# A decoder layer: self-attention's probabilities divided on Vector ahead of their transposes, and the reciprocals of cross-attention moved ahead of two maxima

## What is computed

```python
q = _apply_rope((x @ Wq.T) ...); k = _apply_rope((x @ Wk.T) ...); v = (x @ Wv.T) ...
scores = jnp.einsum('bhqd,bhkd->bhqk', q, k) / np.sqrt(HEAD_DIM)
scores = jnp.where(causal, scores, -jnp.inf)
attn = jax.nn.softmax(scores, axis=-1)
out = jnp.einsum('bhqk,bhkd->bhqd', attn, v)
return out ... @ Wo.T          # then x1 = layernorm(x + this)
```

## Time and profile before

| | |
|---|---|
| median of 3 runs | 1928.02 us (1926.51 to 1933.37) |
| the profiled execution | 1933.5 us, span 1931.7 us |
| busy share of the span | PE 85%, DVE 74%, ACT 73%, POOL 44% |
| self-attention | from 0 to about 638 us |
| cross-attention | to about 1385 us |
| feed-forward | to the end |

### The profile page before, as it was taken

How to read it: one execution, slowest core, us unless ns; L and a number is a source line. 1 busy time by engine, 2 the same in 40 slices (tenths; PEclk the granted TensorE clock), 3 DMA queues, 4 the chain that set the end, 5 groups by cost and what they waited for, 6 DMA issues and landing times. The chain is left out here.

```text
span 1931.7 us, 43922 instructions
## 1 busy us (share of the span) xinstructions
PE 1649.0 (85%) x12964; PEld 904.5 (47%) x13028; DVE 1433.1 (74%) x1915; ACT 1405.0 (73%) x2861; POOL 852.0 (44%) x1378
## 2 busy tenths in 40 slices
PE   5999999999996499999999999998247777777776
PEld 4777777777775133333333333333013333333332
DVE  3555555555554588999999999997558999999986
ACT  4555555555553187888888888887539999999996
POOL 3466565665663322323222323232464554555442
PEclk8999999999998598999999999998668888888887
DMA  3334334334333563444444444444332333333321
GB/s 114 101 97 124 113 110 125 108 111 129 103 114 112 102 188 102 117 109 125 108 110 118 117 116 108 120 109 149 100 96 88 99 109 101 102 110 98 98 66 44
DMA packets 118566, 211.02 MB, mean 109 GB/s; under 512 B 32097, under 2 KB 34689, under 8 KB 116737
## 3 DMA queue, kind: packets, MB, share of 16 engines
q1 hardware_dynamic: 110338, 209.51, 38.4%
q0 software_dynamic: 8192, 1.07, 0.3%
HBM read 133.41 MB, written 76.02 MB: 108 GB/s over the span
## 5 line engine op out<-in xcount | busy, mean ns | idle before, releaser
L926 DVE TENSOR_REDUCE b_smax<-b_m 128x2 f32<-128x1024 f32 x512 | 612.3, 1223 | 75.8 <-PE b_m L981 71.3
L901 ACT ACTIVATE b_prob<-b_e 128x512 f32<-128x512 f32 x1024 | 556.4, 599 | 104.1 <-PE b_e L1028 88.2
L1028 PE MATMUL b_e<-b_xs,b_cs 50*128 50x512 f32 x1024 | 331.0, 479 | 19.5 <-ACT b_prob L901 11.6
L1011 PE MATMUL b_av<-b_prob,b_vT 128*32 128x256 f32 (+1 forms) x3584 | 318.9, 428 | 3.3 <-ACT b_prob L901 0.5
L981 PE MATMUL b_m<-b_cs,b_xs 48*128 48x512 f32 x1024 | 286.5, 445 | 35.9 <-DMA b_gamma<-in_gamma 29.7
L1793 PE MATMUL c_y_ps<-c_w,c_hqT 128*128 128x512 bf16 x481 | 175.3, 531 | 112.6 <-issue 104.7
L1028 PEld LDWEIGHTS b_e<-b_xs,b_cs 50*128 50x128 f32 x1024 | 132.1, 187 | 231.9 <-ACT b_prob L901 205.5
L362 ACT ACTIVATE a_prob<-a_bank,a_neg_max 128x128 f32<-128x128 f32 x512 | 180.0, 388 | 54.5 <-DVE a_neg_max L442 54.5
L852 POOL TENSOR_SCALAR b_max_part<-b_neg_max 16x128 fp32r<-16x128 f32 x64 | 18.6, 291 | 433.6 <-ACT b_neg_max L892 433.6
L1793 PEld LDWEIGHTS c_y_ps<-c_w,c_hqT 128*128 128x128 bf16 x512 | 64.0, 129 | 213.8 <-issue 190.1
L981 PEld LDWEIGHTS b_m<-b_cs,b_xs 48*128 48x128 f32 x1024 | 127.5, 192 | 63.1 <-POOL b_vT L830 30.1
(11 more groups left out here) (149 smaller groups left out, 3174.4 us busy)
## 6 DMA issues: line engine op xcount, KB each, us to landing
scratch_c_part<-a_c_part SPq DMA_DIRECT2D x64, 256.0 KB
scratch_x_part<-a_x_part SPq DMA_DIRECT2D x64, 256.0 KB
b_xs<-scratch_x_part SPq DMA_DIRECT2D x128, 128.0 KB, 3.0
b_cs<-scratch_c_part SPq DMA_DIRECT2D x128, 128.0 KB, 3.0
scratch_heads<-b_heads SPq DMA_DIRECT2D x64, 256.0 KB, 2.2
a_xT<-in_xT SPq DMA_DIRECT2D x32, 256.0 KB, 5.2
a_c_in<-in_ctx SPq DMA_DIRECT2D x32, 256.0 KB, 2.6
a_x<-in_x SPq DMA_DIRECT2D x32, 256.0 KB, 5.3
```

The source lines that it names most:

```text
L901: act.activation(prob[k % 8][:, :], e_ps[bank_of(k)][:, :], ACT.Exp, scale=0.25).then_inc(exp_done, 1)
L926: dve.tensor_reduce(smax[g][:, :, j, qc], m_ps[u % 2][:, :, :], AX.X, ALU.max, negate=True).then_inc(max_done, 1)
L1011: last = pe.matmul(av_ps[2 * XD * h:2 * XD * (h + 1), cols], vT[p][:, lc, XG * g + h, :], prob[(XG * n + 2 * j + e) % 8][:, cols], start=( ...
L1028: pe.matmul(e_ps[bank_of(2 * u + e)][:, :], cs[p][g][half(e), j, lc * P:(lc + 1) * P], xs[p][g][half(e), j, :], start=True, stop=True).the ...
```

## The change

In self-attention the 16 `spread` matmuls, the copy `rdenT`, the single reciprocal and the multiplication of the attended bank are gone. In their place DVE takes, bank by bank, the reciprocals of four sums and multiplies that bank's 128x512 exponentials in SBUF, in place, before PE transposes them. The attended bank is split straight from PSUM. The steps of all engines are written in another order: PE projects q, k and v one after the other, the output projection comes a step later and before the scores, and `attend` stands last. On POOL the power for the standard deviation goes from second place to last, the split of xT from last to third. In cross-attention the two reciprocal instructions stand ahead of the two maxima of the sixth round.

```diff
@@ SP @@
-                if on(4):
-                    b = t - 4
+                if on(5):
+                    b = t - 5
                     sp.wait_ge(x1_split, 2 * b + 2)
...
@@ ACT @@
                     act.wait_ge(prob_tr, 4 * b - 3 + j)
-                    act.wait_ge(rden_done, b)
...
-            def spread_out(b):
-                act.wait_ge(spread_done, b + 1)
-                if later(b):
-                    act.wait_ge(oT_done, b)
-                act.activation(rdenT[:, :, :], v_ps[:, :].rearrange("p (c n) -> p c n", c=KC), ACT.Copy).then_inc(
-                    rdenT_done, 1)
-
             def out_high(b):
-                act.wait_ge(oT_done, b + 1)
+                act.wait_ge(av_done, b + 1)
                 if later(b):
                     act.wait_ge(out_done, b)
-                act.activation(oT_hi[:, :, :], oT[:, :, :], ACT.Copy).then_inc(oT_hi_done, 1)
+                act.activation(oT_hi[:, :, :], o_ps[:, :].rearrange("p (c n) -> p c n", c=KC), ACT.Copy).then_inc(
+                    oT_hi_done, 1)
             def step(t, on):
                 if on(1):
-                    exponentials(t - 1, 2)
+                    values(t - 1)
+                    exponentials(t - 1, 0)
+                    exponentials(t - 1, 1)
                 if on(0):
                     query(t)
                 if on(1):
+                    exponentials(t - 1, 2)
                     exponentials(t - 1, 3)
+                if on(2):
+                    out_high(t - 2)
...
@@ DVE @@
             def out_low(b):
                 dve.wait_ge(oT_hi_done, b + 1)
-                dve.tensor_tensor(oT_lo[:, :, :], oT[:, :, :], oT_hi[:, :, :].bitcast(F32),
-                                  ALU.subtract).then_inc(oT_lo_done, 1)
+                dve.tensor_tensor(oT_lo[:, :, :], o_ps[:, :].rearrange("p (c n) -> p c n", c=KC),
+                                  oT_hi[:, :, :].bitcast(F32), ALU.subtract).then_inc(oT_lo_done, 1)
...
-            def denominators(b):
-                dve.wait_ge(exp_done, 4 * b + 4)
-                if later(b):
-                    dve.wait_ge(spread_done, b)
-                dve.reciprocal(rden[:, :, :], den[:, :, :].rearrange("p j c -> p c j")).then_inc(rden_done, 1)
+            def normalise(b, j):
+
+                dve.wait_ge(exp_done, 4 * b + j + 1)
+                dve.reciprocal(rden[:, j, :], den[:, j, :]).then_inc(rden_done, 1)
+                dve.wait_ge(rden_done, 4 * b + j + 1)
+                dve.tensor_tensor(prob[:, j, :, :], prob[:, j, :, :], rden[:, j, :].unsqueeze(2).broadcast_to([P, KC, P]),
+                                  ALU.mult).then_inc(norm_done, 1)
...
@@ PE @@
-                    pe.wait_ge((qT_done, kT_done, rdenT_done)[n], b)
+                    pe.wait_ge((qT_done, kT_done, v_done)[n], b)
...
             def transpose_prob(b, j):
-                pe.wait_ge(exp_done, 4 * b + j + 1)
+                pe.wait_ge(norm_done, 4 * b + j + 1)
...
-            def spread(b):
-
-                pe.wait_ge(rden_done, b + 1)
+            def attend(b):
+
                 pe.wait_ge(v_done, b + 1)
-                for c in range(KC):
-                    for j in range(HPC):
-                        last = pe.matmul(v_ps[DH * j:DH * (j + 1), c * P:(c + 1) * P],
-                                         rden[:, c, j:j + 1].broadcast_to([P, DH]), ident[:, :],
-                                         start=True, stop=True)
-                last.then_inc(spread_done, 1)
-
-            def attend(b):
-
                 pe.wait_ge(pT_act, 2 * b + 2)
...
@@ cross-attention, DVE @@
                 for n in range(STEPS):
+                    if n == 5 and not first:
+                        reciprocals(t - 1, first=second)
                     if not last:
                         for j in range(2):
                             pair_max(t + 1, 2 * n + j)
-                    if n == 5 and not first:
-                        reciprocals(t - 1, first=second)
```

More of the change, by code:

```diff
@@ L216, in step @@
                             cpart_st, 16)
-                if on(3):
-                    b = t - 3
+                if on(4):
+                    b = t - 4
                     sp.wait_ge(x1_done, b + 1)
@@ L231, in _ @@
             load_weight(3, "woT")
-            for t in range(1, 5):
+            for t in range(1, 6):
                 step(t, lambda k: k <= t)
-            with sp.Fori(5, NB) as t:
+            with sp.Fori(6, NB) as t:
                 step(t, lambda k: True)
-            for t in range(NB, NB + 4):
+            for t in range(NB, NB + 5):
                 step(t, lambda k: t - k < NB)
@@ L391, in step @@
                 if on(1):
+                    exponentials(t - 1, 2)
                     exponentials(t - 1, 3)
-                    values(t - 1)
+                if on(2):
+                    out_high(t - 2)
+                if on(0):
+                    k_transposed(t)
+                if on(1):
                     prob_transposed(t - 1, 0)
-                    prob_transposed(t - 1, 2)
-                    spread_out(t - 1)
+                    prob_transposed(t - 1, 1)
                 if on(0):
                     q_transposed(t)
[L399 to L404, removed]
-            pipeline(act, NB, 1, step)
+            pipeline(act, NB, 2, step)
         @block.vector
@@ L480, in prob_transposed @@
                     pT_dve, 1)
-            def normalise(b):
-                dve.wait_ge(rdenT_done, b + 1)
-                dve.wait_ge(av_done, b + 1)
-                if later(b):
-                    dve.wait_ge(oT_lo_done, b)
-                dve.tensor_tensor(oT[:, :, :], o_ps[:, :].rearrange("p (c n) -> p c n", c=KC),
-                                  rdenT[:, :, :], ALU.mult).then_inc(oT_done, 1)
-            def step(t, on):
+            def step(t, on):
+                if on(1):
+                    maxima(t - 1, 1)
+                    maxima(t - 1, 2)
+                    maxima(t - 1, 3)
+                    normalise(t - 1, 0)
+                    normalise(t - 1, 1)
+                if on(0):
+                    rope_k(t)
+                if on(1):
+                    normalise(t - 1, 2)
+                    normalise(t - 1, 3)
+                if on(2):
+                    out_low(t - 2)
+                if on(1):
+                    prob_transposed(t - 1, 2)
+                if on(3):
+                    norm_x1(t - 3)
+                if on(1):
+                    prob_transposed(t - 1, 3)
                 if on(2):
@@ L609, in step @@
                     project(t, 0)
+                    project(t, 1)
+                    project(t, 2)
                 if on(1):
                     transpose_prob(t - 1, 0)
+                if on(0):
+                    transpose_k(t)
+                if on(1):
                     transpose_prob(t - 1, 1)
-                if on(0):
-                    project(t, 1)
-                if on(1):
                     transpose_prob(t - 1, 2)
-                    transpose_prob(t - 1, 3)
-                    spread(t - 1)
                 if on(0):
                     transpose_q(t)
-                    transpose_k(t)
+                if on(1):
+                    transpose_prob(t - 1, 3)
+                if on(2):
+                    out_projection(t - 2)
+                if on(0):
+                    scores(t)
                 if on(1):
                     attend(t - 1)
-                if on(0):
-                    scores(t)
-                    project(t, 2)
-                if on(1):
-                    out_projection(t - 1)
             pe.wait_ge(const_ld, 16 * CONSTS)
-            pipeline(pe, NB, 1, step)
+            pipeline(pe, NB, 2, step)
 def cross_attention(nc, NB, t_in, scratch, ffn_stage, ffn_abs):
```

37 lines of the change are left out of this document (8 added, 29 removed).

## The result

The changed kernel takes 1916.41 us (median of 7 runs, 1910.24 to 1930.13), against 1932.62 us of the kernel before measured beside it (7 runs). The ratio of the runs is 0.9939, 95% interval 0.9913 to 0.9965: 11.8 us less, between 6.8 and 16.8. Forecast were 24.6 us less. The direction was right and the size twice too large.

What follows compares the result with a forecast made beforehand. PE was taken to bound self-attention; steps fall from 18.30 to 17.7 us, which with an earlier start and 1 us at the end saves 24.6 us: 1928.0 to 1903.4 us, say 1903. Range 1878 to 1925 us.

Steps and rivals of the forecast that it cites:

- floor: Self-attention step on PE without any wait: 16.95 us, 1.35 under now; as a rival 1880 us, chance 0.12.
- Vector's chain before the output projection: Self-attention: DVE's divisions, held by POOL, and the low part make PE wait 0.77 us; step 17.7 us.
- I cost them at nothing: Self-attention: POOL's split of x1 and power moved last, and SP's store a step later, add no time.
- none of these is needed before the same point of the next step: SP's queue in self-attention: later store, x, context's parts and x1 are not needed sooner, so cost 0.
- Start: Start of self-attention: v's projection fills PE's 5.15 us wait, so first scores end near 30.5 instead of 31.45.
- End: After self-attention's last scores: same chain remains, x loaded a little sooner; 1 us gained, between 0 and 3.
- Cross-attention nothing: Cross-attention: moving the reciprocals ahead of the sixth round's maxima gains 0; bounds 15 us gained, 4 us lost.
- the longer chain: Rival, self-attention: a pair costs 0.3 us more or a second POOL instruction gets in; step 18.25, 1920.5 us, chance 0.12.
- The missed gap: Rival, self-attention: POOL's L277 gets in before DVE's L430 and holds it; step 19.1 us, 1947 us, chance 0.13.
- The last sentence of the forecast: Self-attention: wrong as a whole if POOL or SP set the step; PE would wait for q's rotation or xT.

Runs made afterwards that it cites:

- the store first: Changed kernel with SyncE issuing the store of the x parts ahead of the context's load: 1895.86 us, ratio 0.9822 to the kernel before, steps 17.25 us.
- two more powers: Changed kernel with two extra power instructions on GpSimd, into tiles of their own, right ahead of the power: steps 18.77 us on average (one run).

## Why the prediction was right and where it was wrong

- **PE bounds self-attention, and its work falls to a floor**: right. Floor forecast 16.95, measured 16.79 us without the multiplications.
- **Vector's chain before the output projection, held by GpSimd**: right in every link, a little long. The part laid out by hand puts bank 2 at 9.7, bank 3 at 10.8, the low part at 11.5, the output projection at 11.55; with the store first they end at 9.57, 10.59, 11.19 and 11.33 after the start. 17.7 forecast, 17.25 measured: what the forecast computed exists, only in a kernel whose chain is open. Half of the 0.45 us lies ahead of the output projection (0.22), half behind it (5.92 measured, 6.16 forecast).
- **The step that failed** is "I cost them at nothing", on GpSimd's last two instructions and SyncE's store a step later. The sentence names the right risk, a store that lands late and pushes q's rotation, but stops there: it compares the store with the free time of one step and does not follow the queue round to itself. Summed, the chain is 18.02 us, and overrules the 17.7; 31 steps of 17.93 instead of 17.7 are the 7.0 us missing at the last scores. The queue alone would not have shown it: with GpSimd's durations as they are alone the same round adds up to 15.98 us (18.02 less 2.04). The split of x1 and the power were put at 2.5 us and took 3.42, since the divisions hold GpSimd too, which the forecast counted for the rotation only. The argument "none of these is needed before the same point of the next step" was wrong because the split of x1 needs the *landing* of that store, 6.49 us behind its issue.
- **Start**: 30.5 forecast, 29.88 measured, 0.6 us better.
- **End**: forecast 1 us gained, measured 1.6 lost: from the last scores to the stage's end it is 41.65 us now and was 40.05. From the split of x1 of the last batch but one to the end it is 15.9 us in both kernels (from 622.88 before, from 607.30 now). Before, that split stood behind the last batch's power. Now it waits for a store whose data were ready at 595.05, and which SyncE issues at 597.66, behind x's load, which waited for the residual sum (ended at 595.32) of the delayed output projection: the same kind of delay again. The two issues of that store also take 4.81 us instead of the 1.24 of the next one, and why is not shown, so how the 1.6 us divide stays open. The last `attend` waits 0.88 us for that sum too, but the power of its batch is done only behind the split of 607.30:

```profile
595.35 0.34 SPq L207 DMA_DIRECT2D a_x<-in_x  x1
...
597.66 4.81 SPq L201 DMA_DIRECT2D scratch_x_part<-a_x_part  x2
...
607.30 0.62 POOL L244 TENSOR_SCALAR a_x_part<-a_x 128x512 fp32r<-128x512 f32 x1 [10.09 <-DMA scratch_x_part<-a_x_part]
...
615.24 0.62 POOL L244 TENSOR_SCALAR a_x_part<-a_x 128x512 fp32r<-128x512 f32 x1 [5.47 <-DMA scratch_x_part<-a_x_part]
```

- Together: 24.6 forecast, less 7.0 for the step, plus 0.6, less 2.6 for the end is the 15.6 us measured for the stage. The two errors in the step have opposite signs: with the chain open the same change gains 1.8% (ratio 0.9822, some 34 us), more than the 24.6 us forecast.
- **Cross-attention nothing**: right (1.0014; 21.2 us).
- **Rivals**: the longer chain (18.25 us, 1920.5) came nearest in size, by another mechanism. The missed gap did not occur; k's rotation was held by L270 and still came before L273. The last sentence of the forecast, wrong "if the step were set by POOL or SP", was what happened, but PE shows it hardly: its waits are for Vector, since GpSimd's delay reaches PE through the hold.

The Trainium skill, page "SBUF — State Buffer", section "SBUF: two separate sides", counts among the holders of the lock Vector's instructions in a two-port mode, those with two SBUF inputs (against a GpSimd instruction that reads SBUF), and GpSimd's own. The runs agree for two inputs (0.55 us behind L273) and show that the one-input multiplication with a scalar for each row is held as well (3.07 against 0.87 us). By the page it would have to run in a two-port mode; no run here shows whether it does.

## What to carry over

When an edit moves a store in a queue, or what waits for it, follow the chain until it closes: issue to landing, what reuses the buffer, the work up to the wait that stands ahead of the next issue, and sum it; if the sum exceeds the step, it is the step, whatever the engines' own work. Such a chain shows as an engine that waits, step after step, for nothing but the landing of its own last store, with no idle time from there to the next issue, and as an edit that gives nothing until the chain is open. Even steps are no sign of it: they vary from 17.54 to 18.36 us with the chain closed, and by 0.06 with the store first. Sum it with durations as they are beside the other engine, not alone: here that is 18.02 against 15.98. Put a store whose data are ready ahead of a load that waits, and look for the next chain before moving anything past another wait.

## Not expected of the hardware

- The hold between Vector and GpSimd costs both: five of GpSimd's instructions are 2.04 us longer in a round of 18.02 than alone, even a power of 128x1 elements (1.01 instead of 0.55 us); without the divisions the round is 1.24 us shorter.
- Splitting one held instruction into four makes it worse: 3.07 us beside GpSimd, where the four take 0.87 alone and the one piece 1.57 held.
- A store of 2 x 256 KB came back to its waiter 6.2 to 7.4 us after its first issue in the changed kernel's loop, and 5.8 to 7.2 with two more powers.
